# Layer F's operand stacks filled in place, a shorter gate logarithm, and work moved between engines and queues

## What is computed

```python
def attn(x, Wk, bk, Wv, bv, Wf, bf):             # block A, 16 heads
    Q, K, V = split(x), split(x @ Wk + bk), split(x @ Wv + bv)
    attn = softmax(Q @ K.T + mask)
    return x + gelu(attn @ V) @ Wf + bf
def ffn(x, w_q, w_k, w_gate, value_experts, output_experts):   # block F, 8 heads of 64
    q, k = heads(x @ w_q), heads(x @ w_k)
    gates = sigmoid(heads(x @ w_gate))           # 8 experts per head
    gm = one_hot(argmax(gates)) * gates
    values = einsum('bhne,ehdk,bnd->bhnk', gm, value_experts, x)
    out = softmax(causal(q * 0.125 @ k.T)) @ values
    return einsum('bhne,ehkd,bhnk->bhnd', gm, output_experts, out).sum(heads)
x = x + attn(layernorm(x)); x = x + ffn(layernorm(x))
```

## Time and profile before

| what | value |
|---|---|
| median of 3 runs | 1396.0 us (1388.0 to 1396.14) |
| the profiled execution | 1400.44 us |
| its span, first to last instruction | 1398.7 us |
| mean granted TensorE clock | 0.946 |
| busy share of the span | TensorE 85%, VectorE 64%, ScalarE 64%, GpSimd 15% |
| DMA traffic | 106.85 MB |

### The profile page before, as it was taken

How to read it: one execution, slowest core, us unless ns; L and a number is a source line. 1 busy time by engine, 2 the same in 40 slices (tenths; PEclk the granted TensorE clock), 3 DMA queues, 4 the chain that set the end, 5 groups by cost and what they waited for, 6 DMA issues and landing times.

```text
span 1398.7 us, 19702 instructions
## 1 busy us (share of the span) xinstructions
PE 1182.2 (85%) x5720; PEld 652.4 (47%) x5720; DVE 892.7 (64%) x2785; ACT 893.1 (64%) x2551; POOL 203.3 (15%) x262
## 2 busy tenths in 40 slices
PE   2777888888988989888888889888998887988988
PEld 1125643465424754356433564335642465424753
DVE  4626758476674857748476585757758485674855
ACT  2891678727695376944679367782769637695360
POOL 1020111201111011211112011121110201111010
PEclk9997999999999989999899999999999998999999
DMA  6213530064200732026310354005440064200720
GB/s 192 64 64 92 126 104 17 4 152 118 81 2 18 178 92 66 2 56 147 101 50 2 76 137 122 19 4 129 115 104 5 5 163 112 74 2 11 175 53 23
DMA packets 64321, 106.85 MB, mean 76 GB/s; under 512 B 14147, under 2 KB 29891, under 8 KB 63827
## 3 DMA queue, kind: packets, MB, share of 16 engines
q1 hardware_dynamic: 59094, 88.82, 25.1%
q10 hardware_dynamic: 5120, 16.78, 4.7%
HBM read 45.91 MB, written 8.80 MB: 39 GB/s over the span
## 4 chain that ended last, share of the span: by engine, by line
PE 40%; ACT 23%; DVE 15%; issue 12%; DMA 5%; POOL 2%; SPq 1%; ACTq 0%; DVEq 0%; POOLq 0%
ACT masked L825 12%; ACT pt L881 8%; PE ps_m L610 7%; PE ps_o L601 7%; DVE masked L1104 4%; DMA s2q<-mt_f 3%; PE ps_m L436 3%; PE ps_exp L517 3%; PE ps_m L438 2%; PE ps_m L437 2%; PE ps_max L705 2%; PE ps_exp L518 2%; PE ps_exp L436 2%; POOL pt L1002 2%; DVE val L1302 2%
## 5 line engine op out<-in xcount | busy, mean ns | idle before, releaser
L1104 DVE CUSTOM_DVE_ANT_0 masked<-ps_max,mask 128x512 f32<-128x512 f32 (+3 forms) x768 | 352.9, 486 | 220.9 <-PE ps_max L516 86.5
L825 ACT ACTIVATE masked<-masked,low 128x512 f32<-128x512 f32 (+3 forms) x768 | 426.3, 558 | 78.4 <-DVE low L1104 74.1
L881 ACT ACTIVATE pt<-ps_exp 128x384 f32<-128x384 f32 (+1 forms) x480 | 247.5, 522 | 110.3 <-PE ps_exp L518 93.0
L1002 POOL TENSOR_SCALAR_AFFINE_SELECT pt<-pt 128x512 f32<-128x512 f32 (+2 forms) x192 | 133.5, 696 | 714.2 <-ACT pt L881 714.2
L610 PE MATMUL ps_m<-at,oe_sb 128*128 128x512 f32 x416 | 220.1, 618 | 5.5 <-DVE at L1154 3.5
L601 PE MATMUL ps_o<-pt,val 128*32 128x128 f32 (+6 forms) x1536 | 193.4, 473 | 19.9 <-POOL pt L1002 19.3
L516 PE MATMUL ps_max<-s2k,s1q 96*128 96x512 bf16 (+3 forms) x512 | 141.9, 326 | 30.8 <-DMA s2k<-parts_k 17.8
L1154 DVE TENSOR_TENSOR at<-osb,hots 128x512 f32<-128x512 f32 x208 | 145.2, 704 | 15.5 <-PE ps_m L610 15.5
L825 ACT ACTIVATION_READ_ACCUMULATOR masked<-masked,low 128x1 f32 x768 | 149.6, 195 | 0.0
L516 PE MATMUL ps_exp<-s1q,s2k 96*128 96x384 bf16 (+3 forms) x384 | 102.5, 316 | 48.0 <-ACT pt L881 45.1
L517 PE MATMUL ps_exp<-s1q,s1k 128*128 128x256 f32 (+2 forms) x256 | 105.9, 424 | 29.6 <-DMA s2q<-mt_f 23.9
(11 more groups left out here) (156 smaller groups left out, 1765.1 us busy)
## 6 DMA issues: line engine op xcount, KB each, us to landing
s1q<-pt SPq DMA_DIRECT2D x128, 128.0 KB, 2.3
s1k<-pt SPq DMA_DIRECT2D x128, 128.0 KB, 2.3
hots<-hot_d ACTq DMA_DIRECT2D x64, 256.0 KB, 4.3
s1q<-parts_q SPq DMA_DIRECT2D x96, 96.0 KB
s2k<-parts_k SPq DMA_DIRECT2D x96, 96.0 KB
s2q<-pt SPq DMA_DIRECT2D x64, 128.0 KB, 2.3
s2k<-pt SPq DMA_DIRECT2D x64, 128.0 KB, 2.3
parts_q<-pt SPq DMA_DIRECT2D x24, 128.0 KB, 2.3
```

The source lines that it names most:

```text
L825: last = nc.scalar.activation(e, e, ACT.Exp, bias=low[:, g % 2, c:c + 1], scale=-1.0, accum_out=den[:, g % 2, c:c + 1])
L881: nc.scalar.activation(pt[:, (n % 2) * 4 + j, 0:c1 - c0], score_bank(k, u)[:, c0:c1], ACT.Exp).then_inc(exp_done[k].sem, 1)
L1002: nc.gpsimd.affine_select(out=v, in_=v, compare_op=ALU.is_ge, fill=0.0, base=0, pattern=[[0, HG[k]], [0, m], [1, P]], channel_multiplier=- ...
L1104: last = v.tensor_tensor_reduce(out=masked[:, u % JUNK, c0:c0 + w], in0=src[:, c0:c0 + w], in1=mask[:, S - w:S], scale=-1.0, scalar=POS, o ...
```

## The change

- Layer F's stacks: the high halves stay on the partitions where they are. The order of the halves in a stack is turned for odd heads, so that GpSimd copies qh and kh in place into `s1q` and `s1k` (`copy_rows`, 16 copies of 64x512 a batch), ScalarE copies qh and kl into `s2q` and `s2k` (16 copies a batch), and SP sends only ql and the second kh (16 DMAs instead of 48). The maxima and ones rows lie at row 64 for even heads and at row 0 for odd heads; the second product of odd heads reads all 128 rows, that of even heads 66.
- Layer A's products read 72 rows in the maxima pass and 75 in the score pass; the ones rows of `ks` are rewritten with each `restack_k`, and the zero rows of `qs` are gone.
- q/k product u is in bank u % 4.
- Gate: the logarithm of the chosen gate is now minus the logarithm of the smallest 1 + exp(-z), one ScalarE operation; the reciprocal is of 32 columns rather than 256, the gate maximum and three small operations go, and the steps start ahead of the first low half. The last addition of the previous batch's output moves from after low half 0 to after low half 3.
- The next batch's layer norm runs on GpSimd, after the second pair's copies.
- In SP's queue the maxima rows of groups 2 and 3 come between `restack_q` and `restack_k`; at the end of layer A one output product is issued ahead of the last weights product.
- At the start one zero fill of 64 partitions replaces three of 32.

```diff
-BANK.update({("F", "qk", u): u % 2 for u in range(8)})
+BANK.update({("F", "qk", u): u % 4 for u in range(8)})
-NEXT_AT = (7, 11)
+NEXT_AT = 7
@@ SP
-            for dst in (s1q, s2q, s2k):
-                sp.dma_start(dst[64:96].bitcast(F32).rearrange("p h n -> p (h n)"), zeros_d[0].partition_broadcast(32)
-                             ).then_inc(zero_rows.sem, 16)
+            sp.dma_start(s2q[0:64].bitcast(F32).rearrange("p h n -> p (h n)"), zeros_d[0].partition_broadcast(64)
+                         ).then_inc(zero_rows.sem, 16)
...
-                    sp.wait_ge(qk_lo.sem, qk_lo.count(f, 2 * p + 2))
-                    qh, ql, kh, kl = (pt[:, 4 * (p % 2) + n, :] for n in range(4))
-                    for ab in range(2):
-                        r, h = slice(64 * ab, 64 * ab + 64), 2 * p + ab
-                        for dst, src in ((s1q[0:64, h], qh), (s1q[64:128, h], ql), (s1k[0:64, h], kh),
-                                         (s1k[64:128, h], kh), (s2q[0:64, h], qh), (s2k[0:64, h], kl)):
-                            sp.dma_start(dst.bitcast(F32), src[r]).then_inc(pair_sent[p % 2].sem, 16)
+                    ql, kh = (pt[:, 4 * (p % 2) + n, :] for n in (1, 2))
+                    sp.wait_ge(qk_lo.sem, qk_lo.count(f, 2 * p + 1))
+                    for odd in range(2):
+                        sp.dma_start(s1q[ROWS[1 - odd], 2 * p + odd].bitcast(F32), ql[ROWS[odd]]
+                                     ).then_inc(pair_sent[p % 2].sem, 16)
+                    sp.wait_ge(qk_hi.sem, qk_hi.count(f, 2 * p + 2))
+                    for odd in range(2):
+                        sp.dma_start(s1k[ROWS[1 - odd], 2 * p + odd].bitcast(F32), kh[ROWS[odd]]
+                                     ).then_inc(pair_sent[p % 2].sem, 16)
...
                     restack_q(g)
+                    if g < 2:
+                        maxima_rows("F", f, 2 + g)
                     if g == 0:
                         sp.wait_ge(parts_out["k"].sem, parts_out["k"].count(f + 1, 16 * PARTS))
                     restack_k(g)
-                    if g < 2:
-                        maxima_rows("F", f, 2 + g)
@@ TensorE
+            def stacks_made(f, p):
+
+                pe.wait_ge(pair_sent[p % 2].sem, pair_sent[p % 2].count(f, 16 * SENDS * (p // 2 + 1)))
+                pe.wait_ge(rows_copied.sem, rows_copied.count(f, COPIES * (p + 1)))
+                pe.wait_ge(s2q_made.sem, s2q_made.count(f, 2 * (p + 1)))
+                pe.wait_ge(s2k_made.sem, s2k_made.count(f, 2 * (p + 1)))
...
+                if a > 0:
+                    product(a - 1, T * E - TURN)
                 weigh("A", a, NST - 1)
@@ ScalarE
+                        act.wait_ge(rows_copied.sem, rows_copied.count(f, COPIES * (u // 2 - 1)))
...
+                    if u % 2 == 1:
+                        p = u // 2
+                        qh = pt[:, 4 * (p % 2)].bitcast(F32R)
+                        act.wait_ge(qk_hi.sem, qk_hi.count(f, u))
+                        for odd in range(2):
+                            copy(s2q[ROWS[odd], 2 * p + odd], qh[ROWS[odd]]).then_inc(s2q_made.sem, 1)
...
+                    for p in {3: (0, 1), 5: (2,), 7: (3,)}.get(u, ()):
+                        kl = pt[:, 4 * (p % 2) + 3].bitcast(F32R)
+                        act.wait_ge(qk_lo.sem, qk_lo.count(f, 2 * p + 2))
+                        for odd in range(2):
+                            copy(s2k[ROWS[odd], 2 * p + odd], kl[ROWS[odd]]).then_inc(s2k_made.sem, 1)
...
-                        nc.scalar.activation(zabs[:], zabs[:], ACT.Exp, scale=-1.0).then_inc(soft_made.sem, 1)
-                        act.wait_ge(soft_made.sem, soft_made.count(f, 1))
-                        nc.scalar.activation(zabs[:], zabs[:], ACT.Ln, bias=1.0).then_inc(soft_made.sem, 1)
+                        act.wait_ge(gate_step.sem, gate_step.count(f, 2))
+                        nc.scalar.activation(lnw[:].rearrange("p (h t) -> p t h", t=T),
+                                             wlow[:].rearrange("p (t h) -> p t h", t=T), ACT.Ln).then_inc(lnw_made.sem, 1)
@@ GpSimd
+                for t in range(T):
+                    nc.gpsimd.tensor_scalar(xn["A"][:, t, :], x_sb[:, t, :], mv[:, t, 0:1], rstd[:, t:t + 1],
+                                            ALU.subtract, ALU.mult).then_inc(ln_xn["A"].sem, 1)
...
+                for n, (dst, src) in enumerate(((s1q, qh), (s1k, kh))):
+                    if n == 1:
+                        pool.wait_ge(qk_hi.sem, qk_hi.count(f, 2 * p + 2))
+                    for odd in range(2):
+                        nc.gpsimd.tensor_copy(dst[ROWS[odd], 2 * p + odd], src[ROWS[odd]]).then_inc(rows_copied.sem, 1)
+                        pool.wait_ge(rows_copied.sem, rows_copied.count(f, COPIES * p + 2 * n + odd + 1))
@@ VectorE
-                v.tensor_reduce(zmax[:], by_head(ps_m[BANK[("F", "gate", 0)]][:, 0:256]), AX.X, ALU.max
-                                ).then_inc(gate_exp.sem, 1)
-                step(1, v.tensor_scalar(g_w, g_s, 1.0, None, ALU.add))
+                step(1, v.tensor_scalar(g_w, g_s, 1.0, POS, ALU.add, ALU.min))
+                step(2, v.tensor_reduce(wlow[:], by_head(g_w), AX.X, ALU.min))
-                step(2, v.reciprocal(g_s, g_w))
+                step(7, v.reciprocal(gmax[:], wlow[:]))
...
                 gates = gate_ops(f)
+                next(gates)
...
-                    if u == 0 and f > 0:
+                    if u < 3:
+                        next(gates)
+                    if u == 3 and f > 0:
                         outputs_end(f - 1)
-                    if u < 4:
-                        next(gates)
-                        next(gates)
```

More of the change, by code:

```diff
@@ L41 @@
 STACK = PARTS * PARTS * DH
-KROWS = 96
 NEG, POS = -3.0e38, 3.0e38
@@ L346, in maxima_rows @@
             def maxima_rows(k, b, g):
                 sp.wait_ge(t_done[k].sem, t_done[k].count(b, g + 1))
-                for m in range(MROWS[k]):
-                    if k == "A":
+                if k == "A":
+                    for m in range(PARTS):
                         dst, src = qs[STACK + m:STACK + m + 1, 4 * g:4 * g + 4], mt_a[16 * m:16 * m + 16, g % 2]
-                    else:
-                        dst = s2q[64 + m:65 + m, 2 * g:2 * g + 2].bitcast(F32)
-                        src = mt_f[8 * m:8 * m + 8, g % 2]
-                    sp.dma_start(dst.rearrange("o h (t n) -> o (h t) n", n=P), src).then_inc(mrow[k][g % 2].sem, 16)
+                        sp.dma_start(dst.rearrange("o h (t n) -> o (h t) n", n=P), src).then_inc(mrow[k][g % 2].sem, 16)
+                else:
+                    for odd in range(2):
+                        r = X_ROWS[odd]
+                        sp.dma_start(s2q[r:r + 2, 2 * g + odd].bitcast(F32).rearrange("m (t n) -> m t n", n=P),
+                                     mt_f[8 * odd:8 * odd + 8, g % 2]).then_inc(mrow[k][g % 2].sem, 16)
@@ L510, in gates_transposed, with score @@
                 last.then_inc(gt_made.sem, 1)
-            def score(k, dst, h, rows, cols):
+            def score(k, dst, h, rows, cols, extra):
                 (l1, l2), (r1, r2) = rows, cols
                 if k == "A":
-                    return mm(dst, l1[0:KROWS, h, l2], r1[0:KROWS, h, r2], start=True, stop=True)
+                    n = STACK + PARTS if extra else STACK
+                    return mm(dst, l1[0:n, h, l2], r1[0:n, h, r2], start=True, stop=True)
+                n = (slice(0, 66), slice(0, P))[h % 2]
                 mm(dst, l1[0][:, h, l2], r1[0][:, h, r2], start=True, stop=False)
-                return mm(dst, l1[1][0:KROWS, h, l2], r1[1][0:KROWS, h, r2], start=False, stop=True)
+                return mm(dst, l1[1][n, h, l2], r1[1][n, h, r2], start=False, stop=True)
             Q = {"A": qs, "F": (s1q, s2q)}
@@ L712, in turn @@
                 f, first = a - 1, T * E - TURN
-                if f >= 0:
-                    product(f, first)
                 project_back(a, (0, 1, 2))
@@ L1023, in _ @@
                 inverse_deviation("F", b)
-                if b + 1 < B:
-                    inverse_deviation("A", b + 1)
+                for p in range(4):
+                    copy_rows(b, p)
+                    if p == 1 and b + 1 < B:
+                        inverse_deviation("A", b + 1)
+                        normalise_next(b)
                 gated_values(b)
```

124 lines of the change are left out of this document (55 added, 69 removed).

## The result

The changed kernel takes 1349.8 us (1347.5 to 1353.1, four runs); the kernel before took 1395.1 us beside it. The ratio is 0.9688, with a 95% interval from 0.9648 to 0.9727: 3.1% faster, where 1355 us (ratio 0.971) was forecast. The profiled execution has a span of 1345.8 us against 1398.7.

A forecast was written before the change was run, and what follows sets the result against it. No engine bounds it throughout: VectorE limits the experts stage, with holes at its head and in layer F's attention. Stage 24 + maxima rows 14 + prologue 3 = 41 us, forecasting 1355 us, range 1334 to 1384.

The forecast's parts named there:

- The signs: What the new profile would show if the prediction was right (waits, first choice, busy times) or wrong (held VectorE steps, late maxima).
- Head: Start of the experts stage: four banks and shorter gate bring the first choice to 14.9 us, 4.7 us a batch earlier.
- The lock: GpSimd copies at the head hold three two-input VectorE gate steps, 0.35 us each, together 1.0; head gain becomes 3.7 us.
- Copies of ScalarE: Experts stage: sixteen copies, 9.4 us a batch; four delay the maxima's exponentials; 1.0 charged with the bank reuse (0 to 2).
- the layer norm's 0.3: Experts stage: moving the next batch's layer norm from VectorE to GpSimd gives back 0.3 us a batch.
- the rival of 1339 us: Experts stage gives more: lock costs nothing, ScalarE copies hide, full-speed clock helps; 40 us there, with 17; chance 0.17.
- DMAs, "this alone gives 0": SP's sends, 48 to 16 a batch: no listed wait ended by a send, so gain 0, 2 us at most.
- GpSimd: Sixteen copies at 0.7 us and four normalising operations add 14 to 21 us beside 43; nobody waits for it soon.
- Maxima rows: Layer F attention, third group: rows issued ahead of restack_k land earlier; 2.0 us over seven batches, 14 us (0 to 24).
- the exchange with `restack_k`: Rival in layer F's attention: the maxima-rows wait is only exchanged for one on restack_k(0); 27 us won, 1369; chance 0.25.
- Prologue: Program start: one zero fill of 1 MB replaces three of 512 KB; 3 us once (1 to 4).
- Product moved up, rows of products: Output product moved ahead was already hidden: 0, at most 0.9 us either way; changed row counts of products: 0.

The follow-up runs named there:

- e4: Kernel before with every edit of the change except the stacks in place, the rows of the products and the zero fill: 1370.0 us, ratio 0.978.
- e3: Kernel before with four banks for the q/k products and the new gate, including the later output addition: 1383.0 us, ratio 0.9872.
- e9: e4 with the last addition of the previous output back behind low half 0: 1341.7 us, ratio 0.9596.
- e7: e3 with the last addition of the previous output back behind low half 0: 1358.7 us, ratio 0.9693.
- e8: Changed kernel with each of GpSimd's 16 copies a batch made twice: 1351.2 us, ratio 0.963.
- e6: Kernel before with only the stacks in place, the rows of the products and the single zero fill: 1422.4 us, ratio 1.0164.
- e5: Changed kernel with the maxima rows of groups 2 and 3 back behind restack_k in SP's queue: 1361.2 us, ratio 0.9721.
- e11: Changed kernel with the first two broadcasts of hots in layer F issued one unit later: 1344.7 us, ratio 0.9613.
- e1: Kernel before with four banks for the q/k products alone: 1380.6 us, ratio 0.9857.
- e2: Kernel before with the new gate work alone, including the later output addition, banks as before: 1377.4 us, ratio 0.9843.

## Why the prediction held, step by step

**The signs.** Of those that were to show it right, three came: TensorE's wait on `qk_lo` is at most 0.7 us, ScalarE is 74.7 us busier, and there is a new wait on the restack, though of 0.6 us a batch and not 1 to 2. Three missed: the first choice comes at 14.6 us, just ahead of the 15 to 16.5; VectorE is 20.6 us less busy and not 28 (24.1 in e4, which has the same gate and layer norm without the copies); the wait on `mt_f` is 19.7 us and not under 10. None of the signs of being wrong came: no gate step is over 0.72 us, no `COPY_PREDICATED` over 754 ns, VectorE's wait before its fourth maximum is 0.57, and the next maxima come 2.1 us earlier against the first score. So the total held, while several of its parts did not.

**Head.** Right, in mechanism and nearly in size. The replay had 14.9 us without the lock and 15.9 with it; the runs show 14.2 (e3) and 14.6. The wait on `qk_lo` is down to 0.7 us at most. The lock was mis-sized: 1.0 charged, 0.4 measured, since one of the three steps is held by 0.3 us and the other two by under 0.1.

**Copies of ScalarE.** The 75 us were right, their price wasn't. The first exponential of the maxima does stand behind four late copies:

```profile
625.87 1.28 ACT L771 ACTIVATE s2q<-pt 64x512 fp32r<-64x512 f32 x2
627.18 1.29 ACT L771 ACTIVATE s2k<-pt 64x512 fp32r<-64x512 f32 x2
628.49 0.72 ACT L838 ACTIVATE masked<-masked,low 128x512 f32<-128x512 f32 x1
```

Yet first to last choice takes 32.6 us with them and 32.8 in e9 without. The term was 1.0 a batch and measured 0. With the lock at 0.4 and the layer norm's 0.3 that makes 4.6 us for the stage, not 3.0. Here the experts stage went the way of the rival of 1339 us.

**DMAs, "this alone gives 0".** This step failed. It looked for waits on sends in the list of the kernel before, found none, and put the number against the new kernel, in which everything around the sends is earlier by 5 us and their start 1 us later. Without the reduction (e4) the change gives 2.2% and not 3.1%. It also missed that "the output's last addition, moved here" has a store behind it on SP's queue, with the sends behind that; I had counted the addition only as 0.7 us of VectorE. e7 and e9 show this to be worth 24 and 28 us by the medians, 25 and 26 by the ratios. The two misses cancelled, and that was luck: the change contains both the damage and its repair.

**GpSimd.** Right: 620 to 653 ns a copy against 0.7 taken, 794 ns for a layer norm operation, and no one waits, even at twice the work (e8). `COPY_PREDICATED` is not held, 706 to 754 ns. But the reason that stands beside it (one SBUF operand) doesn't carry to other instructions, as e6 shows: `TENSOR_SCALAR` has one input too, and is held.

**Maxima rows.** Right in kind. The wait per batch fell, and the exchange with `restack_k` is there. Booked were 14 us; e5 gives 7.6 by the waits, 11 by the medians and 5 by the ratios. The forecast's "under 10 us in total" for the wait on `mt_f` failed with 19.7: 14 us of it went when the broadcasts no longer lay in front (e11), and 5.6, nearly all of it at the first score, is what moving the rows doesn't touch. The stretch of the attention became 2.1 us shorter, as forecast, but only 0.75 of it goes back in e5. The rest stands beside TensorE's clock: over the six batches the mean granted clock of this stretch was 0.87 before and 0.95 after, and TensorE's busy time in it fell from 20.5 to 19.0 us. The clock is 0.96 in e5 too, so it didn't come from moving the rows; what it came from isn't shown.

**Prologue.** Not seen. The key parts leave at 22.70 us and the first product of layer A starts at 35.77, against 25.25 and 37.27 before; but the first layer A ends at 106.3 to 109.6 us in the six kernels with one zero fill (mean 107.8) and at 104.5 to 110.1 in the eight with three (mean 106.8). The 3 us were 0.

**Product moved up, rows of products.** Both were put at 0, and neither was tried by itself. e4 against e3, and e9 against e7, put the product, the maxima rows and the layer norm together at 13 and 17 us by the medians, 13 and 14 by the ratios. With 5 to 11 for the rows and 2.4 for the layer norm (0.3 a batch is the prediction's, no run shows it alone), 0 to 10 us are left for the product.

**The sum.** 41 us were forecast, 52.9 came between the two profiles and 45 between the medians. The experts stage gave 1.6 a batch more than booked; the prologue gave 3 less, the maxima rows 3 to 9 less; and outside of all my terms a batch wins 1.0 us behind the next maxima and 1.3 of the attention's 2.1, for which no cause is shown. That the total came out 5 us from the median is partly luck: what the stage gave more, these other parts gave less, and the two misses on the sends cancelled.

## To carry to other kernels

Before you call a transfer hidden, replay its deadline in the new schedule: here it was hidden by a stall that the same change removed. When you move an operation to shorten a chain, follow its result to whatever waits for it at the front of an in-order queue; a 0.7 us addition held 24 sends through the store between them, and its place was worth 24 to 28 us. And ask of each part of a change whether it pays by itself or repairs another part: leaving the addition alone beat the whole restacking.

## What the runs showed of the hardware

- A copy on GpSimd holds VectorE's `TENSOR_SCALAR` with one SBUF input: 0.12 us became 0.50, 0.28 became 0.59, four of a layer norm 1.09 became 1.80 (e6). In the changed kernel it held neither `COPY_PREDICATED` (706 to 754 ns) nor, by more than 0.1 us, two of the three gate steps with two SBUF inputs.
- Which steps are held hangs on where they meet a copy. In e6 `osb<-osb,wmax` took 0.66 us in the batches in which it began 0.23 us into a copy, and 0.42 where only 0.1 us of a copy was left; there the next copy took 0.73 us rather than 0.61, and the cast that began inside it 0.59 rather than 0.29. So twice the copies did not hold VectorE twice: it is busy for 872.0 us in e8 and for 872.1 in the changed kernel.
- The stop of TensorE at the head goes with a lower clock. From layer A's end to the first choice TensorE stands for 2.8 us ahead of one product in the kernel before, and in each of the six batches the granted clock falls to the level of 1.2 GHz between 12.5 and 15.6 us after layer A's end, where the stop lies at 10.9 to 13.7; the mean over the stretch is 0.87. With a stop of 3.5 us (e6) it falls in all six as well (0.89), with one of 1.97 (e1) in two of six, and with none over 0.5 us (e2, e3, the changed kernel) in none: there it is 1.00, the level of 2.4 GHz. What this costs in time was not measured by itself.
